# Two early transposes, one router product, one gating step and one addition put at other places in the issue order of a Strassen-Winograd transformer block

## The chip, the cores and the metric

The kernel runs on one core of a Trainium2 chip. The metric is the device time of one execution in microseconds. Before the change it is 2317.74 us, the median of three runs (2317.13 to 2318.90).

## What is computed

Sixteen sequences of 128 tokens and 1024 features pass a gated cross attention (32 query heads, 8 key/value heads of 128) and then a gated mixture of 64 rank-16 experts. All in float32.

```python
x = x + tanh(g_xattn[0]) * xattn(layernorm(x), ctx_4096, mask, q_w, k_w, v_w, o_w, q_norm_w, k_norm_w)
x = x + tanh(g_ffn[0])   * ffn(layernorm(x), A, B, Wr)

# ffn, per token:
scores = xf @ Wr.T                              # 64 experts
top_vals, top_idx = lax.top_k(scores, 16)
G = zeros.at[rows, top_idx].set(softmax(top_vals))
h = einsum('nd,krd->nkr', xf, A)
out = einsum('nkr,kdr->nd', h * G[:, :, None], B) * 2.0
```

## The kernel before

**Products.** Every large matrix product is cut into 96 entries, numbered e. Each entry multiplies 256 rows by one 1024x1024 block with the seven products of the Strassen-Winograd scheme, so an entry is seven "beats" j = 0 to 6, product k on beat j. A product is 4 parts of 3 matmuls of 128x512 (high times high, high times low, low times high), since each float32 operand is split in a rounded half `s_hi`/`t_hi` and a rest `s_lo`/`t_lo`. The stationary side of an entry (`s`) is new for every entry; the moving side (`t`) stays for a set of entries and is replaced at e = 8, 16, ..., 80 and 88.

**Entries.** e = 0 to 15 make keys and values (two sets, the second begins at e = 8), 16 to 47 queries with the attention woven in, 48 to 79 the output projection, `A0` = 80 to 87 the experts' first factor, `B0` = 88 to 95 their second. Pairs of sequences are numbered i = 0 to 7.

**Who does what.** TensorE (PE) runs the products and all transposes. ScalarE (ACT) rounds the halves and empties PSUM bank 0. VectorE (DVE) forms every `s_lo` and `t_lo` (L1320), empties the other banks and combines the seven products. GpSimd (POOL) forms the sums of the stationary side (L1799 to L1805), scales keys (L1830) and gates ranks (L1898). SyncE (SP) issues the DMAs. The order on each engine is written out by hand in one loop per engine and phase, over e and j; an engine never passes an instruction that waits. Semaphores tie the engines together.

**Around the change.** For keys, PE transposes on beat 2 of entry e the key rows of e - 1 (`key_columns`, L786) and the x rows (`x_columns`, L803), and on beat 3 the other half of x. In e = 80 to 87 the router runs after product 3 (`router`, L877) on all of `s`, its transposed scores after product 4 (`score_rows`, L896), then DVE picks the top 16 in four pieces (`choose`, L1538). The resulting gates are multiplied on the ranks of pair i by POOL (`gate`, L1890) in the entry after, PE transposes the four gated tiles on beats 4, 4, 6 and 7 of that entry (`rank_columns`, L907), ACT copies them out a beat later and SP stores them. Tables `GATED_AT`, `COLUMNS_AT`, `COPIED_AT`, `OUT_AT` hold those beats, `tiles_at` (L374) adds the entry. In e = 88 to 95 `y_rows` (L1581) turns the products into output rows: the lower left quarter is `usum` plus product 6, which is on beat 7, i.e. beat 0 of the next entry.

**The turn of an entry.** On beat 5 DVE runs `y_rows(e, 5)` and then `s_lo` 0 and 1 of the next entry, on beat 6 `s_lo` 2 and 3. Product 0 of the next entry waits for `s_lo` 0.

Of the kernel before, what the change touches and what calls it, by code (L numbers as in the profile page):

```python
# [233 lines left out]
def program(nc, d, plan, bank, sem, ctx):  # L234
# [82 lines left out]
    ct = [m.over(name, [P, HALF], rw_at + w * HALF * 4) for w, name in enumerate(("c22", "c12", "c21"))]  # L317
# [55 lines left out]

    def tiles_at(beat, table):  # L374
        found = []
        for i in range(PAIRS):
            at = beat - plan.beat0[A0 + i + 1]
            found += [(i, t) for t in table.get(at, ())]
        return found
# [71 lines left out]
    def _(sp):  # L451
# [186 lines left out]
        def y_rows_out(i, w):  # L638
            sp.wait_ge(y_set, 3 * i + 2 + w)
            if w == 0:  # L640
                sp.wait_ge(taken[0], plan.after[B0 + i, 4])
            sp.dma_start(d.y[tiles(pair_of_output(i))[w]], yr[i % 2][w][:, :]).then_inc(y_out[i % 2], 16)
# [108 lines left out]
    def _(pe):  # L751
# [173 lines left out]
        for e in range(KV0, QA0):  # L925
            for j, k in enumerate(entries[e].ks):
                if e == 0 and k in (1, 2):
                    spare_products(10 if k == 1 else 5)
                product(e, k)
                if e and j == 0 and e == 1:  # L930
                    pe.wait_ge(const_in, 16 * CONSTS)
                if e and j == 2:
                    key_columns(e - 1, 0)
                    x_columns(e - 1, 0)
                if e and j == 3:
                    x_columns(e - 1, 1)
                if e and j == 5:
                    key_columns(e - 1, 1)
# [28 lines left out]
        for e in range(A0, B0):  # L967
            for j in SEVEN:
# [3 lines left out]
                if j == 3:  # L972
                    router(e - A0)
                if j == 4:
# [35 lines left out]
    def _(act):  # L1010
# [282 lines left out]
        for e in range(A0, B0):  # L1293
            for j in SEVEN:
                if j == 0:
                    first_product(e)
                if j == 4:
                    router_scores(e - A0)
# [19 lines left out]
    def _(dve):  # L1318
# [262 lines left out]
        def y_rows(i, j):  # L1581
# [12 lines left out]
            if j == 5:  # L1594
                result12(e, ct[1][:, :])
                dve.wait_ge(taken[2], plan.after[e, 5])
                nc.vector.scalar_tensor_tensor(yr[b][0][:, right], ct[1][:, :], tg2[:, :], yr[b][0][:, right], ALU.mult, ALU.add).then_inc(y_set, 1)
            if j == 7:
                result21(e, ct[2][:, :])
                dve.wait_ge(taken[3], plan.after[e, 6])  # L1600
                nc.vector.scalar_tensor_tensor(yr[b][1][:, left], ct[2][:, :], tg2[:, :], yr[b][1][:, left], ALU.mult, ALU.add).then_inc(y_set, 1)
# [127 lines left out]
        for e in range(A0, B0):  # L1729
            i = e - A0  # L1730
            for j in SEVEN:
# [14 lines left out]
                if j == 5:  # L1746
                    rank_tile(i, 2)
                    choose(i, 0)
# [225 lines left out]
```

## Time and profile before

| | us |
|---|---|
| median of three runs | 2317.74 |
| lowest, highest | 2317.13, 2318.90 |
| the profiled execution | 2318.4 |
| its span, first to last instruction | 2316.6 |
| PE busy | 2261.6 |
| DVE busy | 1597.6 |
| ACT busy | 1183.9 |
| POOL busy | 1144.8 |

The page gives busy time per engine over the whole span, the table of waits says which engine waited for which line, and the timeline lists single instructions with the idle time before them in brackets and what ended it. The profiled execution lies 0.7 us above the median, inside a spread of 1.8 us.

### The profile page before, as it was taken

The numbers are of one execution on the slowest core, as the hardware profiler recorded it, in microseconds if no ns is written. First come the engines' busy times: TensorE is split into PE (matmuls) and PEld (weight loads), VectorE is DVE, ScalarE is ACT, GpSimd is POOL, SyncE is SP. The second block draws the span as 40 slices with busy tenths as digits, with TensorE's granted clock in tenths as the row PEclk, the third lists the DMA queues.
The fourth block names the chain that finished last, engine by engine and source line by source line (L and its number), as shares of the span: only waits on it lengthen the run. The fifth ranks groups of instructions, "written<-read, shape, count | busy, mean of one in ns | idle before, by whom it ended". The sixth has DMA issues, their size and how long they took to land.

```text
span 2316.6 us, 35630 instructions
## 1 busy us (share of the span) xinstructions
PE 2261.6 (98%) x11615; PEld 1906.0 (82%) x11615; DVE 1597.6 (69%) x2669; ACT 1183.9 (51%) x3773; POOL 1144.8 (49%) x1735
## 2 busy tenths in 40 slices
PE   6999999999999999999999999999999999999999
PEld 5887887888888878888888788888888887888787
DVE  7558558777777797777777954755756878555755
ACT  5546546666666676666666732422424335333421
POOL 3666566666555555555555453233232664534221
PEclk9999999999999999999999999999999999999999
DMA  5688466767667367764322635645557566323643
GB/s 198 218 245 296 150 197 232 212 165 204 183 170 191 121 212 205 230 179 128 110 91 92 209 100 164 182 127 166 162 152 216 186 217 255 128 92 136 237 164 136
DMA packets 177062, 408.78 MB, mean 176 GB/s; under 512 B 11824, under 2 KB 77616, under 8 KB 159664
## 3 DMA queue, kind: packets, MB, share of 16 engines
q1 hardware_dynamic: 169392, 351.97, 44.1%
q0 software_dynamic: 7488, 54.53, 12.9%
q8 instruction: 96, 1.57, 0.3%
q14 instruction: 86, 0.70, 0.1%
HBM read 282.72 MB, written 190.84 MB: 204 GB/s over the span
## 4 chain that ended last, share of the span: by engine, by line
PE 84%; DVE 4%; POOL 4%; issue 3%; ACT 3%; DMA 2%; SPq 0%; POOLq 0%; ACTq 0%; DVEq 0%
PE bank L769 23%; PE bank L771 23%; PE bank L770 23%; PE bank L827 4%; PE bank L835 2%; PE bank L815 2%; DVE t_lo L1320 1%; PE bank L852 1%; PE bank L851 1%; PE bank L850 1%; ACT t_hi L1024 1%; POOL s_hi L1811 1%; DVE s_lo L1320 1%; DMA t_raw<-combos 1%; DMA staged<-in_w_q 1%
## 5 line engine op out<-in xcount | busy, mean ns | idle before, releaser
L769 PE MATMUL bank<-t_hi,s_hi 128*128 128x512 f32 x2688 | 1084.0, 403 | 30.7 <-DVE t_lo L1320 17.3
L771 PE MATMUL bank<-t_hi,s_lo 128*128 128x512 f32 x2688 | 1053.8, 392 | 0.0
L770 PE MATMUL bank<-t_lo,s_hi 128*128 128x512 f32 x2688 | 1050.9, 391 | 0.0
L769 PEld LDWEIGHTS bank<-t_hi,s_hi 128*128 128x128 f32 x2688 | 507.2, 189 | 128.1 <-issue 32.3
L771 PEld LDWEIGHTS bank<-t_hi,s_lo 128*128 128x128 f32 x2688 | 505.8, 188 | 110.7
L1320 DVE TENSOR_TENSOR s_lo<-staged,s_hi 128x512 fp32r<-128x512 f32 x672 | 525.0, 826 | 88.9 <-ACT s_hi L1035 86.9
L770 PEld LDWEIGHTS bank<-t_lo,s_hi 128*128 128x128 f32 x2688 | 507.5, 189 | 90.3
L1035 ACT CAST s_hi<-staged 128x512 fp32r<-128x512 f32 x434 | 250.2, 623 | 184.9 <-POOL staged L1801 71.5
L1782 POOL TENSOR_SCALAR small<-small 128x4 f32<-128x4 f32 (+1 forms) x192 | 75.9, 395 | 446.9 <-ACT small L1131 341.4
L1799 POOL TENSOR_TENSOR staged<-staged 128x512 f32<-128x512 f32 x86 | 115.3, 1340 | 365.5 <-DMA staged<-heads 196.9
L1463 DVE SCALAR_TENSOR_TENSOR probs<-bank,small,mask 128x128 f32<-128x128 f32 x512 | 143.9, 343 | 87.1 <-POOL small L1789 43.6
L1137 ACT ACTIVATE probs<-probs,small 128x128 f32<-128x128 f32 x512 | 197.5, 387 | 9.0 <-DVE small L1467 9.0
L1125 ACT ACTIVATE bank<-bank 128x128 f32<-128x128 f32 x512 | 135.4, 265 | 113.9 <-PE bank L815 113.9
L1118 ACT ACTIVATE heads<-bank,small 128x512 f32<-128x512 f32 x128 | 88.2, 689 | 185.1 <-PE bank L852 185.1
L1811 POOL CAST s_hi<-staged 128x512 fp32r<-128x512 f32 x238 | 153.4, 712 | 8.5 <-DVE staged L1335 8.5
L827 PEld LDWEIGHTS bank<-keys,queries 128*128 128x128 f32 x1024 | 133.5, 191 | 13.9 <-issue 4.6
L1320 DVE TENSOR_TENSOR t_lo<-t_raw,t_hi 128x2048 fp32r<-128x2048 f32 x55 | 131.7, 2403 | 10.9 <-ACT t_hi L1024 9.6
L1044 ACT COPY ev<-bank 128x512 f32<-128x512 f32 x96 | 56.1, 584 | 162.1 <-PE bank L771 150.7
L827 PE MATMUL bank<-keys,queries 128*128 128x128 f32 x1024 | 135.2, 275 | 2.2 <-DVE probs L1463 2.1
L1802 POOL TENSOR_TENSOR staged<-staged 128x512 f32<-128x512 f32 x86 | 128.7, 1497 | 0.0
L1805 POOL TENSOR_TENSOR staged<-staged 128x512 f32<-128x512 f32 x86 | 125.5, 1460 | 0.0
L1801 POOL TENSOR_TENSOR staged<-staged 128x512 f32<-128x512 f32 x86 | 116.5, 1355 | 6.7
(143 smaller groups left out, 2894.7 us busy)
## 6 DMA issues: line engine op xcount, KB each, us to landing
heads<-heads SPq DMA_DIRECT2D x128, 256.0 KB, 4.3
staged<-in_w_q SPq DMA_DIRECT2D x32, 768.0 KB, 5.2
staged<-heads SPq DMA_DIRECT2D x32, 768.0 KB, 6.9
sums<-sums POOLq DMA_DIRECT2D x24, 1024.0 KB, 8.0
t_raw<-in_sets SPq DMA_DIRECT2D x20, 1024.0 KB, 7.1
t_raw<-combos SPq DMA_DIRECT2D x19, 1024.0 KB, 8.6
xt<-x_columns SPq DMA_DIRECT2D x8, 1792.0 KB, 6.8
combos<-in_sets POOLq DMA_DIRECT2D x14, 1024.0 KB, 10.2
```

What stands on the lines that cost most here:

```text
L769: nc.tensor.matmul(out, s_hi[w][:, cols], high, start=start, stop=False, skip_group_check=True)
L770: nc.tensor.matmul(out, s_hi[w][:, cols], low, start=False, stop=False, skip_group_check=True)
L771: done = nc.tensor.matmul(out, s_lo[w][:, cols], high, start=False, stop=at == 3, skip_group_check=True)
L827: done = nc.tensor.matmul(bank[6][:, b * S:b * S + S], qt[j][:, b, :], kg[blk][:, b, :], start=True, stop=True)
L1035: nc.scalar.copy(s_hi[k][:, :], staged[:, k, :]).then_inc(s_hi_done, 1)
L1125: done = nc.scalar.activation(bank[4][:, b * S:b * S + S], bank[4][:, b * S:b * S + S], ACT.Square, accum_out=q_ss[w][:, b:b + 1])
L1137: done = nc.scalar.activation(pr[i % 3][:, b, :], pr[i % 3][:, b, :], ACT.Exp, bias=nmax[w][:, b:b + 1], accum_out=rsum[w][:, b:b + 1])
L1320: return nc.vector.tensor_tensor(out, whole, hi.bitcast(FP32), ALU.subtract)
L1463: done = nc.vector.scalar_tensor_tensor(pr[i % 3][:, b, :], bank[6][:, b * S:b * S + S], q_rstd[w][:, b:b + 1], mask[:, :], ALU.mult, ALU.add)
L1802: nc.gpsimd.tensor_tensor(staged[:, 3, :], staged[:, 0, :], staged[:, 3, :], ALU.subtract).then_inc(s_sum, 1)
L1805: nc.gpsimd.tensor_tensor(staged[:, 5, :], staged[:, 4, :], staged[:, 1, :], ALU.add).then_inc(s_sum, 1)
L1811: nc.gpsimd.tensor_copy(s_hi[k][:, :], staged[:, k, :]).then_inc(s_hi_done, 1)
```

## The change

Four edits.

1. In e = 8 and 9 the transposes of the keys and of the first half of x come after product 3 instead of product 2.
2. `router_beat` is 4 for e = 80 and 3 for the others: the first router runs after product 4 instead of 3, its scores are transposed after product 5, ACT copies them after `rank_tile`, and DVE's first piece of `choose` goes from beat 5 to beat 6, behind `s_lo` 0 and 1 of e = 81.
3. `tiles_at` adds one entry more for the last pair: its gating, transposes, copies and store go from e = 88 and the start of 89 to e = 89 and the start of 90.
4. In `y_rows`, `usum` times the gate is added to the lower left quarter on beat 5; product 6 is then scaled and added straight from its bank on beat 7. Before, beat 7 first added `usum` and the bank into a tile `c21` and then scaled and added that.

```diff
+    def router_beat(e):
+        return 4 if e == A0 else 3
+
     def tiles_at(beat, table):
         found = []
         for i in range(PAIRS):
-            at = beat - plan.beat0[A0 + i + 1]
+            at = beat - plan.beat0[A0 + i + (2 if i == PAIRS - 1 else 1)]
             found += [(i, t) for t in table.get(at, ())]
         return found
...
             sp.wait_ge(y_set, 3 * i + 2 + w)
-            if w == 0:
+            if w:
+                sp.wait_ge(taken[3], plan.after[B0 + i, 6])
+            else:
                 sp.wait_ge(taken[0], plan.after[B0 + i, 4])
...
-                if e and j == 2:
+                if e and j == (3 if e in (8, 9) else 2):
                     key_columns(e - 1, 0)
                     x_columns(e - 1, 0)
                 if e and j == 3:
...
-                if j == 3:
+                if j == router_beat(e):
                     router(e - A0)
-                if j == 4:
+                if j == router_beat(e) + 1:
                     score_rows(e - A0)
...
+                if j == router_beat(e) + 1:
+                    router_scores(e - A0)
                 if j == 4:
-                    router_scores(e - A0)
                     rank_tile(e - A0)
...
                 nc.vector.scalar_tensor_tensor(yr[b][0][:, right], ct[1][:, :], tg2[:, :], yr[b][0][:, right], ALU.mult, ALU.add).then_inc(y_set, 1)
+                nc.vector.scalar_tensor_tensor(yr[b][1][:, left], usum[:, :], tg2[:, :], yr[b][1][:, left], ALU.mult, ALU.add).then_inc(y_set, 1)
             if j == 7:
-                result21(e, ct[2][:, :])
-                dve.wait_ge(taken[3], plan.after[e, 6])
-                nc.vector.scalar_tensor_tensor(yr[b][1][:, left], ct[2][:, :], tg2[:, :], yr[b][1][:, left], ALU.mult, ALU.add).then_inc(y_set, 1)
+                dve.wait_ge(prod, plan.prod[e, 6])
+                dve.wait_ge(y_set, 3 * i + 3)
+                nc.vector.scalar_tensor_tensor(yr[b][1][:, left], bank[3][:, :], tg2[:, :], yr[b][1][:, left], ALU.mult, ALU.add).then_inc(taken[3], 1)
...
                 if j == 5:
                     rank_tile(i, 2)
+                if j == router_beat(e) + 2:
                     choose(i, 0)
```

Three places show how rows move. First PE in e = 8, from the end of product 2 to the start of product 4 (`k_normed_85` and `x_rows_82` are the rows of e = 7). Before:

```order
L771 MATMUL bank<-t_hi,s_lo 128x512
L786 MATMUL bank<-ident,k_normed_85 128x128 x4
L803 MATMUL bank<-ident,x_rows_82 128x128 x4
L769 MATMUL bank<-t_hi,s_hi 128x512
...
L803 MATMUL bank<-ident,x_rows_82 128x128 x4
```

After, from the last matmul of product 3:

```order
L777 MATMUL bank<-t_hi,s_lo 128x512
L792 MATMUL bank<-ident,k_normed_85 128x128 x4
L809 MATMUL bank<-ident,x_rows_82 128x128 x8
L775 MATMUL bank<-t_hi,s_hi 128x512
L776 MATMUL bank<-t_lo,s_hi 128x512
```

All twelve transposes now stand together between products 3 and 4; e = 9 reads the same.

Second, DVE at the turn from e = 88 to 89 (`y_rows_144` is the second row tile of the pair, `s_lo` is that of e = 89). Before:

```order
L1356 TENSOR_TENSOR c_148<-bank,usum 128x512
L1597 SCALAR_TENSOR_TENSOR y_rows_143<-c_148,small,y_rows_143 128x512
L1320 TENSOR_TENSOR s_lo<-staged,s_hi 128x512 x4
L1348 TENSOR_TENSOR c_149<-usum,bank 128x512
L1601 SCALAR_TENSOR_TENSOR y_rows_144<-c_149,small,y_rows_144 128x512
L1320 TENSOR_TENSOR s_lo<-staged,s_hi 128x512 x2
```

After:

```order
L1363 TENSOR_TENSOR c_148<-bank,usum 128x512
L1604 SCALAR_TENSOR_TENSOR y_rows_143<-c_148,small,y_rows_143 128x512
L1605 SCALAR_TENSOR_TENSOR y_rows_144<-usum,small,y_rows_144 128x512
L1327 TENSOR_TENSOR s_lo<-staged,s_hi 128x512 x4
L1609 SCALAR_TENSOR_TENSOR y_rows_144<-bank,small,y_rows_144 128x512
L1327 TENSOR_TENSOR s_lo<-staged,s_hi 128x512 x2
```

One instruction has gone from behind the four `s_lo` to ahead of them; the number of instructions is the same. The other entries of this phase read alike.

Third, POOL at the last pair (`ranks_138` to `141`) and the sums for e = 90. Before:

```order
L1898 TENSOR_TENSOR ranks_139<-ranks_139,gates_of_tokens_126 128x512
L1898 TENSOR_TENSOR ranks_140<-ranks_140,gates_of_tokens_126 128x512
L1898 TENSOR_TENSOR ranks_141<-ranks_141,gates_of_tokens_126 128x512
L1799 TENSOR_TENSOR staged<-staged 128x512
L1801 TENSOR_TENSOR staged<-staged 128x512
L1802 TENSOR_TENSOR staged<-staged 128x512
L1805 TENSOR_TENSOR staged<-staged 128x512
```

After:

```order
L1907 TENSOR_TENSOR ranks_139<-ranks_139,gates_of_tokens_126 128x512
L1808 TENSOR_TENSOR staged<-staged 128x512
L1810 TENSOR_TENSOR staged<-staged 128x512
L1811 TENSOR_TENSOR staged<-staged 128x512
L1814 TENSOR_TENSOR staged<-staged 128x512
L1907 TENSOR_TENSOR ranks_140<-ranks_140,gates_of_tokens_126 128x512
L1907 TENSOR_TENSOR ranks_141<-ranks_141,gates_of_tokens_126 128x512
```

The third and fourth tile are gated behind the sums of e = 90 instead of ahead of them; the first two keep their place.

## Rows read from the trace of the kernel before

**Rows 1.** Page, part 1: busy us (share of the span) xinstructions.

```profile
PE 2261.6 (98%) x11615; PEld 1906.0 (82%) x11615; DVE 1597.6 (69%) x2669; ACT 1183.9 (51%) x3773; POOL 1144.8 (49%) x1735
```

**Rows 2.** Waits of PE, whole span: us in total, times, longest us.

```profile
PE bank L916 <- POOL ranks L1898: 2.6, 2, 2.4
```

**Rows 3.** Timeline of PE, e = 8 and 9: start us, us [idle before <-releaser].

```profile
202.94 0.66 PE L786 MATMUL bank<-ident,k_normed 128*128 128x128 f32 x4 [1.43 <-POOL k_normed L1830]
...
204.63 0.48 PE L769 MATMUL bank<-t_hi,s_hi 128*128 128x512 f32 x1
...
217.55 0.50 PE L769 MATMUL bank<-t_hi,s_hi 128*128 128x512 f32 x1 [0.72 <-DVE s_lo L1320]
...
227.73 0.66 PE L786 MATMUL bank<-ident,k_normed 128*128 128x128 f32 x4 [1.72 <-POOL k_normed L1830]
...
228.58 0.47 PE L769 MATMUL bank<-t_hi,s_hi 128*128 128x512 f32 x1
...
231.78 0.47 PE L769 MATMUL bank<-t_hi,s_hi 128*128 128x512 f32 x1
```

**Rows 4.** Windows: us, busy (x) PE, PEld, DVE, ACT, POOL, PEclk, DMA share, GB/s.

```profile
196.20:219.10 22.90, 19.61 (x91) 15.14 (x91) 22.78 (x21) 16.98 (x38) 19.78 (x17) 1.00 0.69 246
...
1957.00:1985.00 28.00, 23.75 (x121) 18.96 (x120) 27.68 (x42) 16.23 (x25) 12.80 (x14) 1.00 0.62 236
2147.00:2179.80 32.80, 29.34 (x131) 23.25 (x130) 32.42 (x50) 17.68 (x24) 8.97 (x4) 0.95 0.61 236
```

**Rows 5.** Timeline of DVE, value rows of e = 8 and 9.

```profile
213.02 0.68 DVE L1352 TENSOR_TENSOR v_rows<-ev,bank 128x512 f32<-128x512 f32 x1
...
231.68 0.69 DVE L1352 TENSOR_TENSOR v_rows<-ev,bank 128x512 f32<-128x512 f32 x1 [4.58 <-PE bank L771]
```

**Rows 6.** Timeline of PE, e = 80: router, row transposes, product 0 of e = 81.

```profile
1968.36 0.38 PE L891 MATMUL bank<-s_hi,router_hi 128*128 128x256 f32 x1 [2.94 <-DVE s_lo L1320]
...
1977.04 1.03 PE L867 MATMUL bank<-ident,x_rows 128*128 128x128 f32 x8
...
1981.58 0.50 PE L769 MATMUL bank<-t_hi,s_hi 128*128 128x512 f32 x1 [0.76 <-DVE s_lo L1320]
```

**Rows 7.** Timeline of DVE, e = 80: normalised rows, two instructions.

```profile
1975.22 3.29 DVE L1515 TENSOR_SCALAR x_rows<-sums,small 128x1024 f32<-128x1024 f32 x2
```

**Rows 8.** Timeline of POOL, e = 88: the gating of the last pair.

```profile
2163.22 8.97 POOL L1898 TENSOR_TENSOR ranks<-ranks,gates_of_tokens 128x512 f32<-128x512 f32 x4 [22.25 <-DVE gates_of_tokens L1578]
```

**Rows 9.** Timeline of DVE, e = 88: what frees bank 2.

```profile
2166.67 0.68 DVE L1356 TENSOR_TENSOR ev<-bank,usum 128x512 f32<-128x512 f32 x1
```

**Rows 10.** Windows, columns as in rows 4: product 5 of e = 88.

```profile
2167.70:2171.50 3.80, 3.79 (x12) 3.06 (x13) 3.76 (x4) 1.10 (x2) 3.80 (x2) 0.58 0.80 309
```

**Rows 11.** Timeline of DVE, turn from e = 89 to 90.

```profile
2194.57 0.87 DVE L1597 SCALAR_TENSOR_TENSOR y_rows<-c,small,y_rows 128x512 f32<-128x512 f32 x1
2195.36 3.58 DVE L1320 TENSOR_TENSOR s_lo<-staged,s_hi 128x512 fp32r<-128x512 f32 x4
```

**Rows 12.** Timeline of POOL, the same turn.

```profile
2194.85 1.74 POOL L1805 TENSOR_TENSOR staged<-staged 128x512 f32<-128x512 f32 x1
```

**Rows 13.** Timeline of PE, product 0 of e = 90, 92 and 95.

```profile
2197.19 0.50 PE L769 MATMUL bank<-t_hi,s_hi 128*128 128x512 f32 x1 [0.67 <-DVE s_lo L1320]
...
2235.43 0.49 PE L769 MATMUL bank<-t_hi,s_hi 128*128 128x512 f32 x1
...
2292.75 0.40 PE L769 MATMUL bank<-t_hi,s_hi 128*128 128x512 f32 x1
```

**Rows 14.** Timeline of DVE, turns to e = 92 and 95, and the end.

```profile
2234.68 2.49 DVE L1320 TENSOR_TENSOR s_lo<-staged,s_hi 128x512 fp32r<-128x512 f32 x4
...
2291.83 2.49 DVE L1320 TENSOR_TENSOR s_lo<-staged,s_hi 128x512 fp32r<-128x512 f32 x4
...
2312.01 0.69 DVE L1348 TENSOR_TENSOR c<-usum,bank 128x512 f32<-128x512 f32 x1 [1.24 <-PE bank L771]
2312.73 0.75 DVE L1601 SCALAR_TENSOR_TENSOR y_rows<-c,small,y_rows 128x512 f32<-128x512 f32 x1
```

More of the change, by code:

```diff
@@ L316, in program @@
           [m.over("y_rows10", [P, HIDDEN], acc_at), m.over("y_rows11", [P, HIDDEN], acc_at + HIDDEN * 4)]]
-    ct = [m.over(name, [P, HALF], rw_at + w * HALF * 4) for w, name in enumerate(("c22", "c12", "c21"))]
+    ct = [m.over(name, [P, HALF], rw_at + w * HALF * 4) for w, name in enumerate(("c22", "c12"))]
     assert end <= nc.sbuf_top, (end, nc.sbuf_top)
```

## The prediction

> **What bounds the kernel now.** I read the shares of busy time first. PE is busy for 2261.6 of 2316.6 us [rows 1]; no matmul is added or dropped, so only the 55 us in which PE stands still can be won, and the table of waits names what ended them. Three of its waits are those that edits 1 to 3 aim at: the transposes of e = 8 and 9 wait 1.43 and 1.72 us for POOL's scaled keys [rows 3], the first router waits 2.94 us for the last `s_lo` [rows 6], and the transposes of gated ranks in e = 88 wait 2.6 us in two places, 2.4 in one [rows 2]. All lie in the first entries of a set, where DVE must also make seven `t_lo`. The next view is therefore how busy DVE is from each wait up to the start of the entry behind it. From 196.2 to 219.1 us it is busy for 22.78 of 22.90, from 1957 to 1985 for 27.68 of 28.00, from 2147 to 2179.8 for 32.42 of 32.80 [rows 4]. The reader should see two things there: DVE is full, and product 0 of the next entry waits for DVE's `s_lo` at the end of the stretch, at 217.55 [rows 3], 1981.58 [rows 6], and again one entry after the third, at 2197.19 [rows 13]. Where DVE has no gap, a wait of PE taken out earlier comes back before that product 0. The exception is e = 9: there DVE itself waits 4.58 us for PE at 231.68 [rows 5].
>
> **Edit 1, e = 8: 0.** The stall is worth 1.43 us, plus 0.84 in the x transposes (204.63 - 202.94 = 1.69 against 228.58 - 227.73 = 0.85 in e = 9) [rows 3]. With product 3 ahead of them PE runs on, but product 6 of e = 8 needs bank 3, which DVE frees with the value rows at 213.02 + 0.68 = 213.70 [rows 5], and product 0 of e = 9 needs the `s_lo` that let it go at 217.55. Neither depends on PE, since DVE does not pause. I take 0; at best 0.1.
>
> **Edit 1, e = 9: -2.0.** The idle time is 1.72 us, and a stop also costs the overlap of one matmul with the next (about 0.2: records of 0.40 us in a row that advances by 0.23, e.g. twelve matmuls and four transposes in 231.78 - 228.58 = 3.20) [rows 3]. By the time product 3 is through, 2.7 us later, the keys are scaled (the wait ended after 1.72). Product 3 needs nothing that is late, DVE waits for it. The transposes moved are the same twelve. Every later step of these entries hangs on PE's products, so the gain should stay: -1.8 to -2.1.
>
> **Edit 2: -0.9.** The router's 2.94 us are not all won. Product 4 now goes first. The row transposes behind product 5 (1977.04) need the first of two normalised rows, which DVE makes from 1975.22 at 1.65 us each, done about 1976.9 [rows 6, 7]. They can move up by 0.1 at most, so product 6 stays where it is, and the 2.94 us reappear as smaller waits ahead of it. What is won comes from the order on DVE: `s_lo` 0 of e = 81 now stands ahead of the first piece of `choose`, and product 0 had waited 0.76 us for it [rows 6]; with the restart 0.9. Behind the displaced pieces on DVE stand ACT's exponentials and `s_lo` 2 and 3, wanted more than 5 us later; that hides them. Nothing moves on SP or POOL. Bounds: 0 if `s_lo` 0 hits a POOL sum, -1.0.
>
> **Edit 3 and 4, turn to e = 89: +0.4.** Product 5 of e = 88 no longer waits for transposes, but it needs bank 2, free at 2166.67 + 0.68 = 2167.35 [rows 9], 0.8 us before it starts now. Behind it DVE is the bound again [rows 4], and DVE gets an instruction more ahead of `s_lo` 0: the early scaling of `usum`. Its nearest row is the same form at the end, 0.75 us [rows 14]; as neighbours on DVE overlap by 0.08 (2194.57 + 0.87 against 2195.36) [rows 11], it costs 0.67. Against it, two of POOL's four gating steps [rows 8] go away from this stretch and hold DVE up less. A full disturbance is 1.09 us (four `s_lo` in 3.58 against 2.49 us) [rows 11, 14], but here the instructions that follow mostly read PSUM; I take 0.3. Bounds -0.4 and +0.7.
>
> **Turn to e = 90: +2.0.** The eight transposes of tiles 0 and 1 leave a stretch in which PE waited anyway and enter e = 89 ahead of product 5, where it does not: 0.85 us at the price of rows 3. The third group falls behind product 6 into a wait, the fourth moves by one whole entry. The early scaling adds 0.67 in front of `s_lo` 0, which already ends last here (0.67 us of wait) [rows 13]. Then the queue of POOL: the sums of e = 90 end about 2196.6 [rows 12], and tiles 2 and 3 are gated only behind them, just when DVE wants to scale twice and make `s_lo` 0. Next to the last sum one `s_lo` already lost 1.09 us. The lost time is between 0 and 1.3 (a little over one POOL instruction more); I take 0.5, since the sums may start earlier with the store of gated columns out of the way.
>
> **Turn to e = 91: +1.1.** The store of gated columns now shares the queue and the engines with the load of e = 91, as it did with that of e = 90; the sums come later and meet DVE's additions, 0 to 1.1 us, I take 0.5. The early scaling costs 0.67 less the slack.
>
> **Turns to e = 92 to 95: +2.6.** Slack is how long `s_lo` 0 is done before PE wants it. For e = 92 it ends at 2234.68 + 0.68 = 2235.36 and product 0 starts at 2235.43; for e = 95 at 2292.51 against 2292.75 [rows 13, 14]. With 0.05 for the release these slacks are 0.02 and 0.19, and the five turns lie between them; I take 0.1. Each turn then waits 0.57 us and pays 0.1 for a first matmul that takes 0.50 instead of 0.40 [rows 13]: four times 0.67. Bounds 2.2 and 2.9. This is the term on which I stake the forecast: the edit saves DVE nothing per entry, it shifts work ahead of what PE waits for.
>
> **The end: -0.7.** After the last product DVE now runs one instruction instead of two; the 0.69 us at 2312.01 go, with 0.03 between them [rows 14]. The last store leaves that much sooner.
>
> **Sum.** 0 - 2.0 - 0.9 + 0.4 + 2.0 + 1.1 + 2.6 - 0.7 = +2.5 us. Against the span of 2316.6 that is 2319.1, against the profiled execution's 2318.4 it is 2320.9, and since that execution lies 0.7 above the median of 2317.74, the median should be 2320.2.
>
> **Rivals.** (a) The early scaling is hidden. If `s_lo` 0 had more room than I read, or the extra transposes fell into waits, the five late turns and part of the turn to 90 would cost nothing: -2.0 - 0.9 - 0.7 and about +1, 2315.1. Against it speaks the slack of at most 0.19 [rows 13, 14]; for it, that I read it from one execution.
>
> (b) Slower by the port. Two gating steps now queue behind the sums in e = 89, and the late load repeats it in e = 90. If DVE and POOL take strict turns there, DVE's two additions and `s_lo` 0 each lose up to 1.3 us: two turns with 1.5 to 2 us more than I took, 2323.5. It decides from the point where POOL's sums end later than DVE's first addition begins, which is so already (2194.85 + 1.74 against 2194.57) [rows 11, 12]. "SBUF — State Buffer" of the Trainium skill, section "SBUF: two separate sides", makes this a rule: the shared port pair is a lock held for a whole instruction, and the loser blocks fully. By that rule, the trace agrees in the 1.09 us, but not on who gets the port next.
>
> (c) Faster: the stalls do vanish. Then e = 8 gives 2.3, e = 9 2.0, the router 3.1, the gated ranks 2.6, and product 5 of e = 88, now at a granted clock of 0.58 for 3.8 us (the lower level, 1.2 GHz, for most of it, after the 2.4 us of idling) [rows 10], another 1.6; with 0.7 at the end 12.3 us: 2305.4. It would need DVE to be less full than rows 4 say. A half of it, 2311, would do for a gain that can be told.
>
> (d) That the change does not do what it says is as good as excluded: the order of instructions on each engine has moved as described, and no instruction is added in number.
>
> **Chances.** A measurement of this kernel can tell about 0.2%, 4.6 us, from no change. Forecast 62% (of it 5 above +4.6 us), (a) 18%, (b) 10%, (c) 7%, others 3%. So faster 0.07, same 0.78, slower 0.15. The forecast's own bounds are about 0 and +5; the range for 8 in 10 takes in most of (a) and the lower half of (b): 2314.8 to 2322.8.
>
> **What the profile after would show.** Right: no wait of PE on scaled keys; in e = 8 PE waits instead before products 4 to 6 and product 0 of e = 9 starts at about 217.5; in e = 9 product 4 starts near 229.7 instead of 231.78. Product 0 of e = 81 starts 2.9 us earlier than before (2.0 of them from e = 9), DVE still full before it. Waits on `s_lo` at every turn from 89 to 95, near 0.6 us each, more at 90 and 91, where a DVE row stretches to over 1 us beside POOL's gating. DVE's last instruction follows the last matmul by 0.4 us and nothing follows it. Wrong: product 0 of e = 9 well before 217, or turns 92 to 95 without a wait.

## The result, and the profile after

The changed kernel takes 2322.33 us in the median of 22 runs, the kernel before 2318.27 on the same chips. The ratio of the two is 1.0015, with a 95% interval of 1.0009 to 1.0021, so 2 to 5 us slower: a slowdown clear of the noise, and still inside the 0.2% (4.6 us) that the prediction counts as no change. One of the 22 runs took 4468.47 us and is left out of the ratio. The forecast was 2320.2 with a range of 2314.8 to 2322.8. It was +2.5 us on a median of 2317.74; measured is +4.1 on one of 2318.27. The profiled execution of the changed kernel took 2323.88 us, its span is 2322.1 (before 2318.4 and 2316.6), and where the forecast's sum said +2.5 for the span, the trace has +5.5. The twelve runs below are about these 3 us, and about the terms that were right.

The page first (busy us, share of the span, instructions), then the waits of PE over the whole span (us in total, times, longest):

```profile
PE 2263.8 (97%) x11615; PEld 1906.0 (82%) x11615; DVE 1593.6 (69%) x2669; ACT 1183.7 (51%) x3773; POOL 1142.8 (49%) x1735
```

```profile
PE bank L775 <- DVE s_lo L1327: 9.6, 10, 3.5
PE bank L775 <- DVE ev L1363: 9.1, 5, 3.2
...
PE bank L873 <- DVE x_rows L1522: 1.1, 1, 1.1
```

PE has the same 11615 instructions as before [rows 1] and yet is busy 2.2 us longer: some of them were slower. No row is left in which PE waits for scaled keys or gated ranks [rows 2, 3]. What grew is the waiting on `s_lo` (line 1320 of before is 1327 now; lines of PE's part are 6 higher). Where it stands the timeline of PE shows (start, us, idle time before it and who ended it), here for e = 8, 9, 80 and 88 and for product 0 of e = 89 to 92 and 95:

```profile
206.71 0.47 PE L775 MATMUL bank<-t_hi,s_hi 128*128 128x512 f32 x1 [0.62 <-issue]
...
210.75 0.47 PE L775 MATMUL bank<-t_hi,s_hi 128*128 128x512 f32 x1 [1.07 <-DVE ev L1363]
...
217.79 0.50 PE L775 MATMUL bank<-t_hi,s_hi 128*128 128x512 f32 x1 [0.70 <-DVE s_lo L1327]
...
230.08 0.47 PE L775 MATMUL bank<-t_hi,s_hi 128*128 128x512 f32 x1
...
1975.03 1.09 PE L873 MATMUL bank<-ident,x_rows 128*128 128x128 f32 x8 [1.08 <-DVE x_rows L1522]
...
2164.69 0.47 PE L775 MATMUL bank<-t_hi,s_hi 128*128 128x512 f32 x1 [2.99 <-DVE ev L1363]
...
2174.29 0.80 PE L775 MATMUL bank<-t_hi,s_hi 128*128 128x512 f32 x1 [3.54 <-DVE s_lo L1327]
2174.88 0.63 PE L776 MATMUL bank<-t_lo,s_hi 128*128 128x512 f32 x1
2175.31 0.63 PE L777 MATMUL bank<-t_hi,s_lo 128*128 128x512 f32 x1
...
2198.61 0.50 PE L775 MATMUL bank<-t_hi,s_hi 128*128 128x512 f32 x1 [0.79 <-DVE s_lo L1327]
...
2219.60 0.50 PE L775 MATMUL bank<-t_hi,s_hi 128*128 128x512 f32 x1 [1.18 <-DVE s_lo L1327]
...
2239.45 0.50 PE L775 MATMUL bank<-t_hi,s_hi 128*128 128x512 f32 x1 [0.49 <-DVE s_lo L1327]
...
2298.79 0.50 PE L775 MATMUL bank<-t_hi,s_hi 128*128 128x512 f32 x1 [0.44 <-DVE s_lo L1327]
```

The reader should see three things. The stall of e = 8 is still there in two pieces, and product 0 of e = 9 starts where it did [rows 3]. From e = 90 on every entry starts with a wait. And the row at 2174.29 is of another kind: it takes 0.80 us, the next ones 0.63 each and follow one another every 0.43 us instead of every 0.23. The granted clock (the column after POOL) says why; the windows are the two idle stretches of e = 88 and the beginning of e = 89:

```profile
2161.70:2164.69 2.99, 0.00 (x0) 0.03 (x1) 2.99 (x3) 0.00 (x0) 2.99 (x2) 1.00 0.83 277
2170.75:2174.29 3.54, 0.00 (x1) 0.00 (x1) 3.50 (x7) 1.38 (x3) 0.00 (x0) 0.90 0.14 54
2174.29:2180.43 6.14, 6.14 (x14) 4.80 (x15) 2.42 (x4) 0.61 (x2) 0.00 (x0) 0.50 0.13 54
```

After the idle 3.54 us, PE works for 6.14 us at a granted clock of 0.50, the lower level (1.2 GHz). In the kernel before the same happens one product earlier, after 2.4 us of idling, in product 5 of e = 88 [rows 10].

**Where the time went.** I take the start of product 0 of each entry from the timeline of PE. The table has the length of each entry in us (to product 0 of the next one; for e = 95 to its last matmul), and under "slow" the matmuls of e = 89 that advance by 0.43 us:

| kernel | e=88 | 89 | slow | 90 | 91 | 92 | 93 | 94 | 95 |
|---|---|---|---|---|---|---|---|---|---|
| before | 26.86 | 20.47 | 0 | 19.18 | 19.06 | 19.16 | 19.06 | 19.10 | 18.84 |
| after | 27.23 | 24.32 | 13 | 20.99 | 19.85 | 19.75 | 19.78 | 19.81 | 18.97 |
| after_again | 27.22 | 21.56 | 0 | 21.05 | 19.76 | 19.66 | 19.71 | 19.64 | 18.96 |
| j_fill_both | 27.23 | 21.63 | 0 | 21.01 | 19.64 | 19.83 | 19.70 | 19.68 | 18.95 |
| c_fill | 27.51 | 21.38 | 0 | 21.00 | 19.75 | 19.64 | 19.73 | 19.65 | 18.95 |
| f_gates_first | 27.52 | 22.90 | 11 | 21.04 | 19.74 | 19.68 | 19.72 | 19.65 | 18.95 |
| a_no_scale | 26.58 | 21.06 | 0 | 20.39 | 19.18 | 19.08 | 19.07 | 19.06 | 18.85 |
| b_no_gate | 27.53 | 23.74 | 10 | 19.78 | 19.74 | 19.65 | 19.77 | 19.69 | 18.99 |
| i_scale_only | 27.52 | 21.00 | 0 | 19.65 | 19.84 | 19.68 | 19.67 | 19.70 | 18.94 |
| d_edits12 | 26.86 | 20.52 | 0 | 19.22 | 19.05 | 19.10 | 19.06 | 19.08 | 18.83 |
| e_late | 26.57 | 22.45 | 6 | 20.44 | 19.21 | 19.07 | 19.06 | 19.04 | 18.82 |
| h_best | 26.86 | 21.97 | 6 | 19.17 | 19.05 | 19.09 | 19.06 | 19.06 | 18.82 |
| k_best_fill | 28.17 | 20.24 | 0 | 19.18 | 19.05 | 19.06 | 19.06 | 19.07 | 18.82 |

At product 0 of e = 88 the changed kernel is 2.80 us ahead (2147.06 against 2149.86). Then it loses 0.37 + 3.85 + 1.81 + 0.79 + 0.59 + 0.72 + 0.71 + 0.13 = 8.97 and wins 0.70 at the end, where DVE runs one instruction after the last matmul instead of two. That is +5.47, of the 5.5 by which the two spans differ.

### The profile page after: what moved, and what is told of

It is laid out like the page before. It is cut to its first block, busy times and chain, and to the rows that moved or that the text cites. A ratio compares the mean times of both kernels' runs of the same rounds, so it can differ in the third digit from the quotient of the medians.

```text
span 2322.1 us, 35646 instructions
## 1 busy us (share of the span) xinstructions
PE 2263.8 (97%) x11615; PEld 1906.0 (82%) x11615; DVE 1593.6 (69%) x2669; ACT 1183.7 (51%) x3773; POOL 1142.8 (49%) x1735
## 4 chain that ended last, share of the span: by engine, by line
PE 85%; DVE 5%; issue 3%; POOL 3%; ACT 3%; DMA 2%; SPq 0%; ACTq 0%; POOLq 0%; DVEq 0%
PE bank L775 23%; PE bank L777 23%; PE bank L776 23%; PE bank L833 4%; PE bank L841 2%; PE bank L821 2%; DVE t_lo L1327 2%; PE bank L858 1%; PE bank L857 1%; PE bank L856 1%; ACT t_hi L1030 1%; DMA t_raw<-combos 1%; DVE s_lo L1327 1%; POOL s_hi L1820 1%; DMA staged<-in_w_q 1%
## 5 line engine op out<-in xcount | busy, mean ns | idle before, releaser
L1327 DVE TENSOR_TENSOR s_lo<-staged,s_hi 128x512 fp32r<-128x512 f32 x672 | 519.5, 817 | 100.6 <-ACT s_hi L1041 98.7
```

The lines of the kernel that those rows point to most:

```text
L1327: return nc.vector.tensor_tensor(out, whole, hi.bitcast(FP32), ALU.subtract)
```

## The experiments

Each kernel ran 11 times, beside 33 runs of the kernel before, in three groups. In these before had medians of 2318.47, 2318.52 and 2318.61 us, so medians can be compared across the groups to about 1 us. From each kernel there is one profile; what differs between executions of one program can be told only where a kernel has two (the changed one, as after and after_again) or from the medians.

| kernel | what it has | median | ratio to before (95%) |
|---|---|---|---|
| d_edits12 | edits 1, 2 | 2314.46 | 0.9987 (0.9978-0.9996) |
| a_no_scale | edits 1, 2, 3 | 2317.39 | 0.9996 (0.9987-1.0005) |
| b_no_gate | edits 1, 2, 4 | 2319.16 | 1.0004 (0.9996-1.0013) |
| c_fill | after, 12 spare matmuls | 2320.07 | 1.0009 (1.0001-1.0018) |
| e_late | after, early scaling behind `s_lo` 0, 1 | 2316.49 | 0.9991 (0.9982-0.9999) |
| h_best | d_edits12, early scaling behind `s_lo` 0, 1 | 2314.49 | 0.9982 (0.9973-0.9990) |
| i_scale_only | edit 4 | 2323.04 | 1.0019 (1.0010-1.0027) |
| f_gates_first | after, POOL gates ahead of its sums | 2320.74 | 1.0007 (0.9998-1.0016) |
| after_again | after | 2322.07 | 1.0015 (1.0007-1.0024) |
| j_fill_both | after, 24 spare matmuls | 2319.97 | 1.0008 (0.9999-1.0017) |
| k_best_fill | h_best, 10 spare matmuls | 2315.00 | 0.9985 (0.9976-0.9994) |
| g_e8_only | edit 1 at e = 8 alone | 2318.71 | 1.0001 (0.9992-1.0009) |

### The four edits apart

**Edits 1 and 2 alone (d_edits12).** The kernel before with

```diff
-                if e and j == 2:
+                if e and j == (3 if e in (8, 9) else 2):
                     key_columns(e - 1, 0)
                     x_columns(e - 1, 0)
...
-                if j == 3:
+                if j == router_beat(e):
                     router(e - A0)
...
```

> The kernel before with edits 1 and 2 alone. Theory of the prediction: e = 9 gives 1.7 to 2.0 us, the turn to e = 81 another 0.9 to 1.0, e = 8 nothing; 2.6 to 2.9 us under the kernel before, 2315.5. Rival (the gain is given back later, at the turns behind e = 88 where DVE is full): under 1 us, 2317.5.

Measured: 2314.46, 4.0 us under before (by the ratio 0.9 to 5.1), and every entry from e = 88 on as long as before within 0.06 us. The first two edits are a gain, and what they win is not given back. The profiles account for 2.8 of it, 1.98 in e = 9 and 0.83 from product 0 of e = 80 to that of e = 82; the rest of the 4.0 is not placed, and may be noise.

**Edit 1 at e = 8 alone (g_e8_only).**

```diff
-                if e and j == 2:
+                if e and j == (3 if e == 8 else 2):
                     key_columns(e - 1, 0)
                     x_columns(e - 1, 0)
```

> The kernel before with edit 1 at e = 8 alone: there the transposes of keys and x stand behind product 3 instead of 2, nothing else is changed. Theory (DVE has no gap up to product 0 of e = 9, the stall moves to the waits on banks and comes back): product 0 of e = 9 starts at 217.5 within 0.3 us, the median equals that of before within 0.5 us. Rival (the 1.43 us and the 0.84 of the x transposes are won): product 0 of e = 9 at 215.3 to 216.1, the median 1.4 to 2.3 us lower.

Measured: ratio 1.0001. In its timeline of PE

```profile
206.37 0.47 PE L773 MATMUL bank<-t_hi,s_hi 128*128 128x512 f32 x1 [0.62 <-issue]
...
210.42 0.47 PE L773 MATMUL bank<-t_hi,s_hi 128*128 128x512 f32 x1 [1.04 <-DVE ev L1361]
...
217.45 0.50 PE L773 MATMUL bank<-t_hi,s_hi 128*128 128x512 f32 x1 [0.70 <-DVE s_lo L1325]
```

the stall on the keys has become two waits on banks, and product 0 of e = 9 starts at 217.45 against 217.55 [rows 3]. DVE is busy for 22.76 of the 22.90 us up to there, as before [rows 4]. The rival, 1.4 to 2.3 us, is refuted.

**Without edit 4 (a_no_scale)** and **without edit 3 (b_no_gate)**, each the changed kernel with that edit undone:

```diff
-                nc.vector.scalar_tensor_tensor(yr[b][1][:, left], usum[:, :], tg2[:, :], yr[b][1][:, left], ALU.mult, ALU.add).then_inc(y_set, 1)
             if j == 7:
...
+                result21(e, ct[2][:, :])
```

```diff
-            at = beat - plan.beat0[A0 + i + (2 if i == PAIRS - 1 else 1)]
+            at = beat - plan.beat0[A0 + i + 1]
```

> The changed kernel without edit 4: beat 7 adds usum and the bank first and scales then, as before the change. Theory 1 (the early scaling stands ahead of s_lo 0 at every turn of an entry): the waits of PE on s_lo at the turns to e = 92 to 95, 0.38 to 0.49 us each in the changed kernel, vanish, the turns together give back 2.8 us, the turns to 89, 90 and 91 another 0.6 each or more, and the end loses 0.6; in all 3.5 to 5 us under the changed kernel (2322.3), 2317.5 to 2319. Rival, the port between DVE and POOL is what costs: the turns to 90 and 91 keep nearly all their loss and the total falls by under 3 us.

> The changed kernel without edit 3: the last pair is gated, transposed and stored in e = 88 and at the start of 89, as before the change. Theory 1 (moving it lets PE finish e = 88 early, so that it idles 3.5 us in one piece before product 0 of e = 89 and runs that product at half clock where nothing hides it): the 14 slow matmuls of e = 89 (0.43 us a piece instead of 0.23, 2.8 us) are gone, slow ones may come in e = 88 where DVE is late anyway; total 1 to 2 us above the kernel before, 2319.5. Rival (the port and the transposes alone cost): the slow matmuls in e = 89 stay or cost nothing, the total falls by 1 us only, 2321.3.

Measured: 2317.39 and 2319.16. The first lies just below the range of its theory (2317.5 to 2319): the waits at the turns to 92 to 95 are gone, and the whole falls by more than the 3 us of the rival. The median of b_no_gate came as expected, its mechanism did not: with edit 3 undone e = 89 still has 10 slow matmuls. The table of lengths separates the two edits. Edit 3 (a_no_scale against d_edits12) gives 0.28 us in e = 88 and costs 0.54 in e = 89 and 1.17 in e = 90. Edit 4 (i_scale_only against before, both with the gating where it was) costs 0.66 in e = 88, 0.53 in e = 89, 0.47 in e = 90 and 0.52 to 0.78 in each of the next four.

**Edit 4 alone (i_scale_only)**: the kernel before with the early scaling and the new last addition.

```diff
+                nc.vector.scalar_tensor_tensor(yr[b][1][:, left], usum[:, :], tg2[:, :], yr[b][1][:, left], ALU.mult, ALU.add).then_inc(y_set, 1)
             if j == 7:
-                result21(e, ct[2][:, :])
...
```

> The kernel before with edit 4 alone (the early scaling of usum ahead of s_lo 0, and the end shorter by one instruction). Theory: no difference up to e = 88; then 0.5 to 0.8 us at each of the turns to e = 90 to 95, 0.3 to 0.7 at the turn to 89, 0.6 us back at the end: the span is 3 us longer than before, the median 2321 to 2322, ratio 1.0013. If the scaling ahead of the turn to 89 lets PE idle long enough for the clock to fall in e = 89, up to 2 us more. Rival (edit 4 is free, edit 3 is what costs): no waits on s_lo at e = 92 to 95, a median of 2317.7.

Measured: 2323.04, 4.5 us over before, somewhat more than expected. That edit 4 is free is refuted. Edit 4 is the largest loss of the four; summed in medians, edits 1 and 2 give 4.0, edit 4 costs 4.5, and edit 3 costs 2.9 (2317.39 - 2314.46), 2.0 (2316.49 - 2314.49) or 3.2 (2322.33 - 2319.16), each of these to about 2 us.

### Where the early scaling stands (e_late, h_best)

Both have the early scaling on beat 6 instead of 5, so that DVE makes `s_lo` 0 and 1 of the next entry first (two instructions later; the recorded text below calls it two beats); h_best also has the gating where it was.

```diff
                 nc.vector.scalar_tensor_tensor(yr[b][0][:, right], ct[1][:, :], tg2[:, :], yr[b][0][:, right], ALU.mult, ALU.add).then_inc(y_set, 1)
+            if j == 6:
                 nc.vector.scalar_tensor_tensor(yr[b][1][:, left], usum[:, :], tg2[:, :], yr[b][1][:, left], ALU.mult, ALU.add).then_inc(y_set, 1)
```

> The changed kernel with one edit undone in its place alone: the early scaling of usum (half a row of the second output tile) stands on DVE two beats later, behind s_lo 0 and 1 of the next entry instead of ahead of them. Work is the same. Theory (the early scaling costs because it stands ahead of s_lo 0, for which PE waits at each turn): the waits on s_lo before product 0 of e = 92 to 95 go (0.3 to 0.5 us each, with the slower first matmul 2.8 us in all), and about as much again at the turns to 89 to 91, while the 0.6 us at the end stay: the profiled span falls by 3 to 5 us against the changed kernel's 2322.1, to 2317 to 2319, the median to 2318 to 2319. If the clock drops behind product 5 of e = 88 as it did there, 2 to 3 us of that are missing again in e = 89. Rival (what costs is that DVE has one instruction more beside POOL or DMA, wherever it stands): waits of the same length turn up at other products, and the span stays within 1 us of 2322.

> Edits 1 and 2 as in the changed kernel, the gating of the last pair where it was before, and the early scaling two beats later on DVE, behind s_lo 0 and 1 of the next entry. Theory: edits 1 and 2 are worth 2.7 us, edit 3 is best left out, and the early scaling costs nothing in this place and gives 0.6 us at the end: a median 0.4 to 0.8 us below the kernel with edits 1 and 2 alone (2314.46), so about 2313.9, ratio 0.998. Rival: the scaling only shifts DVE's delay to product 1 or 2 of the next entry: then 2315 to 2318.

Measured: 2316.49, 5.8 us under the changed kernel and so more than the 3 to 5 that were expected, and 2314.49. DVE in e_late at the turn to e = 92 (L1606 is the early scaling):

```profile
2233.41 1.01 DVE L1604 SCALAR_TENSOR_TENSOR y_rows<-c,small,y_rows 128x512 f32<-128x512 f32 x1
2234.35 1.28 DVE L1327 TENSOR_TENSOR s_lo<-staged,s_hi 128x512 fp32r<-128x512 f32 x2
2235.55 0.74 DVE L1606 SCALAR_TENSOR_TENSOR y_rows<-usum,small,y_rows 128x512 f32<-128x512 f32 x1
2236.21 1.28 DVE L1327 TENSOR_TENSOR s_lo<-staged,s_hi 128x512 fp32r<-128x512 f32 x2
```

Product 0 of e = 92 to 95 has no wait there, and the entries are back at 19.04 to 19.07. The same instruction with the same data costs nothing behind `s_lo` 0 and 1, and 0.5 to 0.8 us per entry ahead of them: in the entries e = 91 to 94 the place costs, not the work. The rival (waits of the same length elsewhere) is refuted. Against d_edits12 the later scaling should have won another 0.4 to 0.8 us; it did not show in the median (2314.49 against 2314.46), while the ratios to before, 0.9982 and 0.9987, cannot tell the two apart. h_best is, with d_edits12, the fastest kernel of this study, 4 us under before.

### The port between POOL and DVE (f_gates_first)

The changed kernel, but POOL gates all four tiles of the last pair in e = 88, ahead of its sums of e = 90.

```diff
-            for i, t in tiles_at(beat, GATED_AT):
+            for i, t in [(i, t) for i, t in tiles_at(beat, GATED_AT) if i < PAIRS - 1] + \
+                    ([(PAIRS - 1, t) for t in range(4)] if beat == plan.beat0[B0] + 4 else []):
```

> The changed kernel, but POOL gates all four tiles of the last pair in e = 88, one behind the other and ahead of its sums of e = 90; the PE transposes of the gated ranks stay where edit 3 put them. Theory (the queue of POOL costs: two gating steps behind the sums hit DVE's two scalings and s_lo 0 at the turn to 90): the early scaling there takes under 1 us instead of 1.55 and 1.78, product 0 of e = 90 and 91 come 0.5 to 1.0 us earlier together, counted from the product 0 before. Rival (the turn to 90 is dear because of the clock alone): the turn stays at 3.9 us where the first matmuls of e = 89 advance by 0.43 us, and at 1.0 where they advance by 0.23 us, whatever POOL does.

Measured: 2320.74, 1.3 us under after_again. DVE and POOL at the turn to e = 90, first in after_again, then in f_gates_first:

```profile
2191.50 1.10 DVE L1604 SCALAR_TENSOR_TENSOR y_rows<-c,small,y_rows 128x512 f32<-128x512 f32 x1
2192.53 1.54 DVE L1605 SCALAR_TENSOR_TENSOR y_rows<-usum,small,y_rows 128x512 f32<-128x512 f32 x1
...
2191.00 1.06 POOL L1907 TENSOR_TENSOR ranks<-ranks,gates_of_tokens 128x512 f32<-128x512 f32 x1
...
2192.01 1.51 POOL L1907 TENSOR_TENSOR ranks<-ranks,gates_of_tokens 128x512 f32<-128x512 f32 x1
```

```profile
2194.40 0.75 DVE L1604 SCALAR_TENSOR_TENSOR y_rows<-c,small,y_rows 128x512 f32<-128x512 f32 x1
2195.07 0.75 DVE L1605 SCALAR_TENSOR_TENSOR y_rows<-usum,small,y_rows 128x512 f32<-128x512 f32 x1
...
2192.57 1.30 POOL L1814 TENSOR_TENSOR staged<-staged 128x512 f32<-128x512 f32 x1
```

With nothing on POOL beside them the two scalings take 0.75 us each, with the two gating steps 1.10 and 1.54: against a POOL that is idle there the late gating costs DVE 0.35 + 0.79 = 1.14 us, and PE 0.83 us of wait before product 0 of e = 90, which f_gates_first does not have (0.29 of it is paid in its e = 88, 27.52 against 27.23 us). The rows also show how: each stretched DVE row ends 0.54 to 0.55 us after the end of the POOL row that it overlaps (2192.60 after 2192.06, 2194.07 after 2193.52), as does the stretched first `s_lo` of before, 2195.36 + 1.78 = 2197.14 after 2194.85 + 1.74 = 2196.59 [rows 12]. "SBUF — State Buffer" of the Trainium skill, section "SBUF: two separate sides", says that of a DVE instruction with two SBUF inputs and a GpSimd instruction that reads SBUF the one that starts first has the shared pair of ports for its whole length, and the other blocks until then; by that rule, the trace agrees in these three pairs. The e = 89 of f_gates_first is still 22.90 us long: the 11 slow matmuls cost 0.2 us each, 2.2 in all, which leaves 20.7 against 21.56. So both causes are real and they add: the queue of POOL 0.8 us against an idle POOL (not against the kernel before, see below), the clock more than that. e = 90 is not helped (21.04).

### The clock in e = 89

Theory: the long entry e = 89 is the low clock, which follows the idle time behind product 6 of e = 88, and not the order of the instructions.

**Spare matmuls (c_fill, j_fill_both).** The changed kernel with 12 more matmuls into a free bank behind product 6 of e = 88; in j_fill_both 12 more behind product 4 as well. Their results are not used.

```diff
                 rank_columns(plan.beat0[e] + j)
+                if e == B0 and j in (4, 6):
+                    for _ in range(12):
+                        nc.tensor.matmul(bank[4][:, :], t_hi[0][:, 0, 0:P], t_hi[0][:, 0, :], start=True, stop=True)
```

> The changed kernel with 12 matmuls of 128x512 more behind product 6 of e = 88, which write a PSUM bank that nobody reads: 2.7 us of work in the 3.5 us in which PE idles there. Theory 1 (the clock falls after that idling): product 0 of e = 89 starts no later and its matmuls follow each other by 0.23 us instead of 0.43, all of e = 89 ends 2.8 us earlier in the profile; the time falls by 1.5 to 2.8 us to about 2320, and its spread from run to run (5.7 us in the changed kernel, 2.5 before) shrinks to about 2.5. Rival (the clock has nothing to do with it, or the loss comes from elsewhere): the time is as in the changed kernel or longer.

> The changed kernel with 24 spare matmuls of 128x128 by 128x512 in e = 88, whose results nobody reads: 12 behind product 4, where PE idled 2.99 us before product 5, and 12 behind product 6, where it idled 3.54 us before product 0 of e = 89. Theory: without the idling no stretch of e = 88 or 89 has a granted clock under 1.00, e = 89 is 21.4 us long as with 12 spare matmuls, and the median is 2319.5 to 2320.3, 1.5 to 2.5 below the changed kernel on this chip. Rival (the clock falls for another reason, the load of DMA or of the other engines, say): 6 to 13 slow matmuls as before, and the median of the changed kernel.

Measured: 2320.07 and 2319.97; after_again, on the chip of j_fill_both, 2322.07. In j_fill_both

```profile
2160.98 2.88 PE L989 MATMUL bank<-t_hi 128*128 128x512 f32 x12
2164.10 0.47 PE L775 MATMUL bank<-t_hi,s_hi 128*128 128x512 f32 x1 [0.24 <-DVE ev L1366]
...
2170.01 2.88 PE L989 MATMUL bank<-t_hi 128*128 128x512 f32 x12
2173.70 0.50 PE L775 MATMUL bank<-t_hi,s_hi 128*128 128x512 f32 x1 [0.82 <-DVE s_lo L1330]
```

the idle times of 2.99 and 3.54 us have shrunk to 0.24 and 0.82, and the granted clock is 1.00 over both stretches, in the places where it was 0.50 in after and 0.58 in after_again:

```profile
2163.50:2168.50 5.00, 4.70 (x20) 3.33 (x19) 4.96 (x6) 0.62 (x1) 0.77 (x1) 1.00 0.81 301
2173.70:2179.20 5.50, 5.50 (x24) 4.53 (x25) 3.68 (x6) 2.15 (x4) 0.00 (x0) 1.00 0.15 60
```

More work on PE makes the kernel 2.1 us faster in the median, and c_fill, with half of it, reads the same to 0.1 us. What carries this are the medians; a single profile with a full clock in e = 89 would not, since after_again has one without spare matmuls. c_fill's own profile does not show it: in that execution the clock had fallen already in product 5 of e = 88, before the spare matmuls.

**The changed kernel again (after_again)**, without any edit.

> The changed kernel once more, word for word, on the same chip as the next two. Theory (a fall of the clock in e = 89 that moves with the execution): the length of the entry e = 89, from its product 0 to that of e = 90, is 21.4 us plus about 0.2 for each matmul that advances by 0.43 instead of 0.23 us; the number of such matmuls is another than the 13 of the first profile, and the rest of the turns (20.99, 19.85, 19.75, 19.78, 19.81) repeat within 0.15 us. Median 2321 to 2322.5. Rival (the long e = 89 belongs to the order of the instructions): 24.3 us and 13 slow matmuls again.

Measured: 2322.07 in the median, but its profiled execution took 2319.7 us, with a span of 2317.8 instead of 2322.1, and shows

```profile
2163.57 0.47 PE L775 MATMUL bank<-t_hi,s_hi 128*128 128x512 f32 x1 [2.99 <-DVE ev L1363]
...
2173.17 0.50 PE L775 MATMUL bank<-t_hi,s_hi 128*128 128x512 f32 x1 [2.28 <-DVE s_lo L1327]
```

```profile
2164.00:2168.00 4.00, 4.00 (x13) 3.09 (x12) 3.96 (x5) 0.62 (x1) 0.00 (x0) 0.58 0.74 286
2173.17:2179.30 6.13, 6.13 (x27) 5.05 (x28) 4.02 (x7) 2.15 (x4) 0.00 (x0) 1.00 0.13 54
```

The same program, instruction for instruction, has its slow stretch here in product 5 of e = 88, where DVE is the bound (e = 88 takes 27.22 us as in the other execution, 27.23), and none in e = 89, which takes 21.56 instead of 24.32. The rival, that the long entry belongs to the order, is refuted. The other turns repeat within 0.17 us. The idle time in front of e = 89 belongs to the same choice: it is 2.28 us where product 5 was slow and 3.54 where it was not. What the clock costs is therefore a matter of where it falls: nothing in e = 88, 2.8 us in e = 89. "TensorE: Matmul & The Clock Gate" of the Trainium skill, section "Part 1: The HAM clock gate (the "warmup" mystery)", says of the slow matmuls at the start of a kernel that one and the same kernel shows 6, 11 or 14 of them from run to run. Here the slow stretch lies inside the kernel, and the two executions agree with that in kind, with 13 and 0 in e = 89.

**Spare matmuls in the best kernel (k_best_fill)**: h_best with ten of them behind product 6 of e = 88, the edit as above.

> Edits 1 and 2, gating where it was, the early scaling behind s_lo 0 and 1, and 10 spare matmuls behind product 6 of e = 88. Without them this kernel idled 2.44 us before product 0 of e = 89 in its profile, and 6 matmuls of e = 89 ran at half the clock. Theory: e = 89 takes 20.5 us as in the kernel with edits 1 and 2 alone, and the median is 0.5 to 1.2 us below that without spare matmuls (2314.49), about 2313.7. Rival (the fall mostly comes earlier in e = 88, where DVE is the bound, so there is little to win): 2314.5.

Measured: 2315.00, no gain over 2314.49; the expectation was wrong. e = 89 did get its 20.24 us. But the clock fell earlier in that execution, at a granted clock of 0.66 from 2164.00 to 2168.80, so product 6 ended later, and the spare matmuls then stood in front of product 0:

```profile
2173.37 2.54 PE L989 MATMUL bank<-t_hi 128*128 128x512 f32 x10
2175.76 0.39 PE L775 MATMUL bank<-t_hi,s_hi 128*128 128x512 f32 x1
```

e = 88 took 28.17 instead of 26.86 us. A filler pays only where PE would certainly idle that long; here it takes with one hand the 1.3 us that it gives with the other.

## Why the prediction was right, and where it was not

The median lies 2 us above the forecast and inside its range, and the sign and the class are right. By its own steps:

- **Edit 1, e = 8: 0.** Right: the changed kernel has 217.79 for 217.55, g_e8_only 217.45, ratio 1.0001. The reasoning (DVE has no gap, so the stall returns before product 0) is shown, not only argued.
- **Edit 1, e = 9: -2.0.** Right: from 0.24 us behind to 1.70 ahead (230.08 against 231.78), -1.94, and 1.77 ahead is kept up to e = 80.
- **Edit 2: -0.9.** Right: 1.77 ahead before, 2.80 behind e = 81, -1.03. As said, the router's wait came back in pieces (1.08 us before the row transposes at 1975.03).
- **Turn to e = 89: +0.4.** Right: 26.86 to 27.23. a_no_scale and i_scale_only show its parts, -0.28 for the gating and +0.66 for the scaling, where I had -0.3 and +0.67.
- **Turn to e = 90: +2.0.** This is the step that failed, in both directions. Without the clock it was too dear: 21.56 - 20.47 = +1.09 in after_again. The turn can be split at the DVE row that reads product 5, which waits for PE. First before, then after_again:

```profile
2176.72 0.50 PE L769 MATMUL bank<-t_hi,s_hi 128*128 128x512 f32 x1 [0.84 <-DVE s_lo L1320]
...
2193.84 0.69 DVE L1356 TENSOR_TENSOR c<-bank,usum 128x512 f32<-128x512 f32 x1 [1.97 <-PE bank L771]
...
2195.36 1.78 DVE L1320 TENSOR_TENSOR s_lo<-staged,s_hi 128x512 fp32r<-128x512 f32 x1
```

```profile
2190.77 0.69 DVE L1363 TENSOR_TENSOR c<-bank,usum 128x512 f32<-128x512 f32 x1 [2.87 <-PE bank L777]
...
2194.73 0.50 PE L775 MATMUL bank<-t_hi,s_hi 128*128 128x512 f32 x1 [0.83 <-DVE s_lo L1327]
```

  From product 0 of e = 89 to that row it was 17.12 us and is 17.60, from there to product 0 of e = 90 it was 3.35 and is 3.96. PE's part is therefore +0.48, where I had +0.85: eight transposes come in ahead of product 5, but the four that stood behind product 0 of e = 89 have left, and I did not take them off. DVE's part is +0.61, which is the 0.67 of the scaling and nothing for POOL, where I had +0.5. The kernel before paid there already: `s_lo` 0 lost 1.1 us (1.78 for 0.68) and the scaling 0.12 (0.87 for 0.75) beside the last sum of POOL. In after_again that sum starts 1.56 us sooner after product 0 of e = 89 and is out of the way, and the 1.14 us beside the gating stand in its place. The parts simply add: a_no_scale has +0.59, i_scale_only +0.53, together 1.12.

  And one term was missing: in the profiled execution +2.8 us for a clock that falls behind the idle time in front of e = 89. I had read the low clock of product 5 of e = 88 [rows 10] and used it only in rival (c), as something that might go. In neither execution of the changed kernel did it go, it landed at another place; under DVE's work it cost nothing. Taking PE's work out of e = 88 (edit 3), making `s_lo` 0 later (edit 4) and a product 5 at the full clock together made the idle time in front of e = 89 3.54 us long. b_no_gate and h_best show that edit 3 is not needed for a fall there: their slow matmuls in e = 89, 10 and 6, followed idle times of 3.10 and 2.44 us.
- **Turn to e = 91: +1.1.** Too low: +1.81, and +1.87 in after_again. The scaling's 0.6 was right. For the rest I had 0.5, and edit 3 alone has 1.17 (20.39 in a_no_scale against 19.22 in d_edits12). Split at the same DVE row it is 0.44 on PE, where the fourth group of transposes now opens e = 90, which I did not charge, and 0.72 on DVE, which now meets POOL's last sum for e = 91: there the port costs more than I took.
- **Turns to e = 92 to 95: +2.6.** Right: +0.79, +0.59, +0.72, +0.71, together 2.8, by the waits and first matmuls of 0.50 us that were named. The late place in e_late takes all four away. The stake of the forecast, that the slack of `s_lo` 0 is the price, is shown.
- **The end: -0.7.** Right: -0.72 in the profile of after.

In the first profiled execution the sum is off by +5.5 - 2.5 = 3.0, of it 1.85 in the turn to 90, 0.7 in the turn to 91 and 0.4 in small pieces. In the median only part of the clock's cost shows, since the fall comes at another place in some executions; filling the idle time gives back 2.1 us. So the median lies near the forecast partly by luck: the two errors of e = 89, 0.9 too dear and a missing term of up to 2.8, have opposite signs.

Of the rivals, (a) is refuted by i_scale_only and (c) by g_e8_only for e = 8 and by the table of waits for the rest. (b), 2323.5, came close for other reasons: its mechanism exists, and the two engines do take turns in the rows above, but against the kernel before the port costs nothing in the turn to 90 and 0.7 us in the turn to 91, together less than the two times 0.5 of the sum.

Open: what decides whether the clock falls in product 5 of e = 88, in e = 89 or not at all. i_scale_only idled 3.10 us ahead of e = 89 and showed no slow matmul; b_no_gate, with the same order of instructions in e = 88 and 89 and the same 3.10, had 10. Open too is a difference of 1.2 us from product 0 of e = 32 to that of e = 36, which take 124.20 us in the profile of before and 124.26 in that of after, and 122.9 to 123.1 in all twelve later profiles. It touches no edit, but it makes those profiles look faster than before by 1.2 us, and lengths of entries are compared here for that reason, not spans.

## What to carry to other kernels

Work that an engine has to do anyway is not free to move: ask what stands behind it in the queue and who waits for that, and put it behind the last instruction that somebody waits for. Where one engine is full, taking work from its partner makes the partner idle longer, and for PE an idle stretch is not neutral; look where the slow matmuls lie now, and ask on which side of the bound they will lie afterwards. Before summing terms of one stretch, split it at the row where one engine waits for the other, and ask of each part what leaves it as well as what enters, and what the old order already pays there: a price read from a full disturbance is not an extra if the kernel before has that disturbance in the same place.

## What the runs showed of the hardware

PE can be slowed by having less to do: 24 spare matmuls, 5.8 us of work, made the kernel 2.1 us faster. The place of the fall differs between executions of one program: 13 slow matmuls in e = 89 in one, none in another, with otherwise equal turns, and 4.2 us between the two executions, 2.8 of them from this and 1.2 from the stretch behind e = 32 that stays open. And a pair of instructions of DVE that read and write SBUF takes 0.75 + 0.75 us alone and 1.10 + 1.54 beside two gating steps of POOL (1.06 and 1.51 us); each of the two ends 0.54 to 0.55 us after the POOL instruction beside it.
